# Cross-attention's DMA queue: a context chunk's transposing load directly behind its low part, ahead of the next context rows

## The chip, the cores and the metric

One core of a Trainium2 chip runs the kernel. The metric is the time of one execution in device microseconds (us); three executions of the kernel before took 1845.61 to 1848.7, with a median of 1846.81. Engines: TensorE (PE; its weight loads are PEld), VectorE (DVE), ScalarE (ACT), GpSimd (POOL) and SyncE (SP), which here issues nearly all DMAs. SPq in a row is SyncE's sequencer issuing one.

## What is computed

One decoder layer with the normalisation behind each part, on x (16 batches, 112 rows, 1024 columns) and a context (16 batches, 375 rows, 1024 columns), all in float32:

```
x = layernorm(x + attn(x))                    # q, k, v of width 256
x = layernorm(x + xattn(x, ctx))              # the part around the change
x = layernorm(x + ffn(x))                     # 1024 -> 2752 -> 1024, 4-bit weights, silu(gate) * up

xattn(text, features):
    Q = text @ Wq.T + bq;  K = features @ Wk.T + bk
    return softmax(Q @ K.T / sqrt(1024)) @ features
```

## The kernel before

The kernel writes each engine's instruction stream by hand; engines meet through semaphores, and within an engine order is the order written. To keep float32 accuracy with float16 matmuls it splits an operand into a high part (float16 of the scaled value) and a low part (what is left), and multiplies in three passes (high high, high low, low high).

Cross-attention is done one batch n at a time, 16 batches in all. Wq and Wk are multiplied together once into M, so that a batch's logits are (M x1) times the context. G = M x1 is made for pairs of batches in groups called g_chunk, four of them per batch, two batches ahead of use. The context of a batch has 375 rows, taken as three chunks of 128, 128 and 119 rows. For each chunk of each batch:

- SyncE loads the rows from DRAM (load_ctx, L2152; the third chunk as two DMAs, L2155 and L2156) into cx. There is one cx buffer per chunk, so the load of batch n+2 waits until the low part of the same chunk of batch n+1 has been made (semaphore s_cl).
- VectorE takes the largest absolute value of each row (context_max, L779); when all three chunks are there, TensorE and VectorE make a scale out of it (context_largest, context_factor).
- ScalarE writes the high part (context_hi, L1433), VectorE the low part (context_lo, L810), into cxp, which has two slots by the batch's parity.
- SyncE issues a transposing load from cxp to cxt, also two slots (load_cxt, L2178, a DMA_TRANSPOSE of 128 rows by 2048 float16, 512 KB). TensorE's logits (L1784; its matmuls show under the helper's line L1647) wait for all three of a batch (s_ct). The untransposed cxp is what the attended rows are made from.

VectorE's order while batch n is attended: normalise batch n-1, with the low part of chunk 0 of batch n+1 set in while a reciprocal root is fetched from GpSimd; low part of chunk 1 of n+1; softmax input of n (L771), which waits for the logits of n; low part of chunk 2 of n+1; largest of chunk 0 of batch n+2 (waits for its load); row_term of n+1; low part of the probabilities (L816), on which TensorE's attended rows wait; largest of chunks 1 and 2 of n+2; residual sum of batch n (add_attended, L901), which waits for the attended rows; scale of n+2. 

TensorE's order: logits of n, two g_chunks, transposed probabilities, a g_chunk, attended rows, the largest of the context of n+2 (L1744), a g_chunk.

SyncE's order for batch n is the function cross_attention that the diff touches (L2220). Before: for each chunk wait for its low part of n+1 and load the rows of batch n+2 into its place (after chunk 0 also store x2 of batch n-1, L2197); then wait for the logits of batch n-1, and issue the three transposing loads of batch n+1; then the transposing load of x2 of batch n-1 (L2202), the residual rows of batch n+2 (L2144), which wait for the residual sum of batch n, and in batches 0 to 2 two transposing loads of x1 (L2085). Batches 0 to 3 and 12 to 15 are written out, 4 to 11 are a loop of two turns of four. Batches 14 and 15 have no batch n+2 and load no context.

Of the kernel before, what the change touches and what calls it, by code (L numbers as in the profile page):

```python
# [40 lines left out]
def decoder_layer(nc, t_in, out):  # L41
# [19 lines left out]
    CC = len(CP)  # L61
# [28 lines left out]
    with ExitStack() as ctx:  # L90
# [289 lines left out]
        def rows(ap, n):  # L380

            return ap[bass.ds(n * S, S), :]
# [21 lines left out]
        def known(n, limit):  # L404

            return isinstance(n, int) and n < limit


        def batches(g, has):

            for b in range(GB):
                n = g * GB + b
                yield b, n, (lambda k, b=b: has or b + k < GB)
# [1630 lines left out]
        def _(sp):  # L2044
# [37 lines left out]
            def load_x1t(q):  # L2082

                for m in range(2 * q, 2 * q + 2):
                    sp.dma_start_transpose(x1t.rearrange("p l k t -> p (l k) t")[:, :, m * S:(m + 1) * S],  # L2085
                                           x1p_d[m * S:(m + 1) * S, :]).then_inc(s_x1t[q], 16)
# [56 lines left out]
            def load_residual(n, b):  # L2143
                sp.dma_start(xr3[0:S, b % 2, :], rows(x1_d, n)).then_inc(s_xr3[b % 2], 16)  # L2144
# [3 lines left out]
            def load_ctx(n, c):  # L2148

                base = n * CTX + c * P  # L2150
                if c < CC - 1:
                    sp.dma_start(cx[:, c, :], ctx_rows[bass.ds(base, P), :]).then_inc(s_cx[c], 16)  # L2152
                    return
                even = CP[c] // 16 * 16
                sp.dma_start(cx[0:even, c, :], ctx_rows[bass.ds(base, even), :]).then_inc(s_cx[c], 16)  # L2155
                sp.dma_start(cx[even:CP[c], c, :], ctx_rows[bass.ds(base + even, CP[c] - even), :]).then_inc(s_cx[c], 16)  # L2156
# [19 lines left out]
            def load_cxt(c, s):  # L2176

                sp.dma_start_transpose(cxt[s].rearrange("p l k t -> p (l k) t")[:, :, c * P:(c + 1) * P],  # L2178
                                       cxp[s][:, c, :, :].rearrange("p l d -> p (l d)")).then_inc(s_ct[s], 16)
# [14 lines left out]
            def store_x2(n, s):  # L2194

                sp.wait_ge(s_n, NB + n + 1)
                sp.dma_start(rows(x2_d, n), yo[0:S, s, :]).then_inc(s_yout[s], 16)  # L2197

            def load_x2t(n):

                sp.wait_ge(s_lo, n + 1)
                sp.dma_start_transpose(x2t.rearrange("p l k t -> p (l k) t")[:, :, bass.ds(n * S, S)],  # L2202
                                       x2p[0:S, :, :].rearrange("p l d -> p (l d)")).then_inc(s_x2t, 16)

            def load_chunk(i, s, w):

                for m, name in enumerate(("gate", "up")):

                    to = qw[s][m][:, 0:w] if w == P else qw[s][0][:, m * w:(m + 1) * w]
                    if known(i, 1):  # L2210
                        to = qw_first[m]
                    sp.dma_start(to, t_in[f"L0_ffn_{name}_qweight"][:, bass.ds(i * P, w)].bitcast(
                        U32)).then_inc(s_qw[s], 16)
                for r in range(4):
                    for lo, hi in ((0, 3 * GU), (3 * GU, 4 * GU)):
                        at = 0 if lo == 0 else P
                        sp.dma_start(tabc[s][32 * r + lo:32 * r + hi, :, at:at + w],
                                     tabr_d[:, lo:hi, bass.ds(i * P, w)].rearrange("m g c -> g m c")).then_inc(s_tc[s], 16)

            def cross_attention(g, more):  # L2220
                for b, n, has in batches(g, more):
                    if known(n, NB) and n == NB - 2:
                        load_chunk(0, 0, P)
                    for c in range(CC):
                        if has(1):
                            sp.wait_ge(s_cl, CC * (n + 1) + c + 1)
                        if has(2):
                            load_ctx(n + 2, c)
                        if c == 0 and not known(n, 1):
                            store_x2(n - 1, (b + 1) % 2)  # L2230
                    if has(1):
                        if not known(n, 1):
                            sp.wait_ge(s_l, n)
                        else:
                            sp.wait_ge(s_v, 2 * NG)
                        sp.sem_inc(s_due, 1)
                        for c in range(CC):
                            load_cxt(c, (b + 1) % 2)
                    if not has(1):
                        sp.wait_ge(s_l, NB)  # L2240
                        load_chunk(1, 1, P)
                    if not known(n, 1):
                        load_x2t(n - 1)
                    if has(2):
                        sp.wait_ge(s_y3, 2 * (n + 1))
                        load_residual(n + 2, (b + 2) % GB)
                    if known(n, 3):
                        load_x1t(5 + n)

            cross_attention(0, True)  # L2250
            with sp.Fori(1, NG - 1) as g:
                cross_attention(g, True)
            cross_attention(NG - 1, False)


# [186 lines left out]
```

## Time and profile before

| | |
|---|---|
| Median of 3 executions | 1846.81 us |
| Profiled execution | 1848.76 us, span 1847.0 us |
| PE busy | 1737.1 us, 94% of the span |
| DVE busy | 1069.9 us, 58% |
| ACT, POOL busy | 494.4 and 502.6 us, 27% each |
| TensorE's granted clock | 0.99 of full speed |
| Chain that ended last | PE 45%, issue 28%, DVE 11%, SPq 6%, DMA 5% |
| SPq L2178 (the transposing loads of the context) in that chain | 4% |

The span is read as busy time by engine and as a chain. Busy time says how full an engine is on average over stages that are limited by different things; the chain follows back from the last instruction to what released each step. The cross-attention stage runs from about 350 to 700 us. A wait in a row names the producer whose signal came last. Times of rows are microseconds from the start of the span; a mean of one instruction is in ns where it says so.

### The profile page before, as it was taken

The numbers are of one execution on the slowest core, as the hardware profiler recorded it, in microseconds if no ns is written. First come the engines' busy times: TensorE is split into PE (matmuls) and PEld (weight loads), VectorE is DVE, ScalarE is ACT, GpSimd is POOL, SyncE is SP. The second block draws the span as 40 slices with busy tenths as digits, with TensorE's granted clock in tenths as the row PEclk, the third lists the DMA queues.
The fourth block names the chain that finished last, engine by engine and source line by source line (L and its number), as shares of the span: only waits on it lengthen the run. The fifth ranks groups of instructions, "written<-read, shape, count | busy, mean of one in ns | idle before, by whom it ended". The sixth has DMA issues, their size and how long they took to land.

```text
span 1847.0 us, 26676 instructions
## 1 busy us (share of the span) xinstructions
PE 1737.1 (94%) x9784; PEld 979.2 (53%) x9784; DVE 1069.9 (58%) x1656; ACT 494.4 (27%) x734; POOL 502.6 (27%) x326
## 2 busy tenths in 40 slices
PE   5898899897899988998999999999999899999998
PEld 3666644486777754444444444444445344444443
DVE  7788550656788875667777777787775211111111
ACT  3222210354555543233323323233232100000000
POOL 0221378223333425543323223223231000000000
PEclk9999999999999999999999999999999999999999
DMA  9342571599999977763231321322313822122120
GB/s 324 102 130 80 158 205 34 120 209 231 225 236 239 232 166 156 179 143 80 56 88 48 81 62 48 95 48 62 81 45 79 324 101 107 53 106 106 53 106 23
DMA packets 335590, 231.89 MB, mean 126 GB/s; under 512 B 288224, under 2 KB 302624, under 8 KB 333348
## 3 DMA queue, kind: packets, MB, share of 16 engines
q1 hardware_dynamic: 329284, 227.85, 47.8%
q10 hardware_dynamic: 6240, 3.15, 0.6%
q8 instruction: 43, 0.70, 0.2%
q14 instruction: 23, 0.19, 0.0%
HBM read 122.93 MB, written 60.83 MB: 99 GB/s over the span
## 4 chain that ended last, share of the span: by engine, by line
PE 45%; issue 28%; DVE 11%; SPq 6%; DMA 5%; POOL 3%; ACT 1%; DVEq 0%; POOLq 0%; ACTq 0%
PE psum L1647 44%; SPq L2178 4%; DMA arena<-arena 3%; DMA arena<-in_x 2%; DVE arena L810 1%; POOL small L1162 1%; POOL arena L1171 1%; PE psum L1899 1%; PE psum L1825 1%; DVE arena L1016 1%; DVE arena L1014 1%; DVE arena L1011 1%; DVE arena L875 1%; DMA x_parts_scratch<-arena 1%; SPq L2085 1%
## 5 line engine op out<-in xcount | busy, mean ns | idle before, releaser
L1647 PE MATMUL psum<-arena 128*128 128x448 f16 (+6 forms) x7176 | 1273.0, 338 | 50.7 <-DMA arena<-arena 24.6
L1647 PEld LDWEIGHTS psum<-arena 128*128 128x128 f16 (+3 forms) x7176 | 752.3, 109 | 552.8 <-issue 89.4
L2002 PE MATMUL psum<-arena 128*128 128x512 f16 x1820 | 393.5, 379 | 6.4 <-DMA arena<-down_weights_scratch 3.7
L2002 PEld LDWEIGHTS psum<-arena 128*128 128x128 f16 x1820 | 177.7, 98 | 222.2 <-DMA arena<-down_weights_scratch 5.4
L1245 POOL TENSOR_TENSOR arena<-arena 128x1024 f16<-128x1024 f32 (+1 forms) x60 | 149.8, 2509 | 417.0 <-ACT arena L1456 417.0
L1144 DVE SCALAR_TENSOR_TENSOR arena<-psum,small,arena 128x512 f32<-128x512 f32 x28 | 20.9, 751 | 331.9 <-PE psum L2002 331.9
L1162 POOL TENSOR_TENSOR small<-small 112x1 f32<-112x1 f32 (+1 forms) x46 | 50.9, 1107 | 510.7 <-DVE small L471 510.7
L1547 ACT ACTIVATE arena<-arena,small 128x448 f32<-128x448 f32 x68 | 45.5, 668 | 208.6 <-DVE arena L1076 145.2
L1456 ACT ACTIVATE arena<-arena 128x1024 f16<-128x1024 f32 (+1 forms) x60 | 68.8, 1173 | 120.2 <-DVE arena L852 91.9
L1236 POOL TENSOR_TENSOR arena<-arena 128x224 f16<-128x224 f32 x64 | 55.6, 869 | 124.9 <-ACT arena L1427 124.8
L850 DVE TENSOR_TENSOR arena<-arena,psum 128x1024 f32<-128x1024 uint32 x65 | 79.1, 1217 | 2.9 <-PE psum L1825 0.9
L852 DVE TENSOR_TENSOR arena<-arena,psum 128x1024 f32<-128x1024 f32 x65 | 79.3, 1221 | 2.2
L1475 ACT ACTIVATE arena<-arena 128x448 f16<-128x448 f32 (+1 forms) x88 | 50.7, 576 | 103.7 <-DVE arena L864 103.7
L875 DVE TENSOR_TENSOR arena<-arena 128x448 f16<-128x448 f32 (+1 forms) x88 | 56.8, 646 | 36.8 <-ACT arena L1475 36.8
L779 DVE TENSOR_REDUCE small<-arena 128x1 f32<-128x1024 f32 (+1 forms) x48 | 58.0, 1216 | 26.5 <-DMA arena<-in_ctx 26.1
L810 DVE SCALAR_TENSOR_TENSOR arena<-arena,small 128x1024 f16<-128x1024 f32 (+1 forms) x48 | 61.2, 1279 | 12.0 <-ACT arena L1433 12.0
L1433 ACT ACTIVATE arena<-arena,small 128x1024 f16<-128x1024 f32 (+1 forms) x48 | 51.8, 1138 | 46.3 <-DVE small L806 46.3
L466 DVE BATCH_NORM_STATS2 small<-arena 112x6 f32<-112x512 f32 (+1 forms) x92 | 58.8, 681 | 1.4 <-DVE small L806 1.1
L482 DVE TENSOR_SCALAR arena<-arena,small 112x1024 f32<-112x1024 f32 (+1 forms) x46 | 44.3, 964 | 25.1 <-POOL small L1162 25.1
L864 DVE SCALAR_TENSOR_TENSOR arena<-arena,small 128x448 f32<-128x448 f32 (+1 forms) x72 | 49.0, 680 | 13.4 <-ACT arena L1484 10.6
L830 DVE TENSOR_TENSOR arena<-arena,small 128x1024 uint32<-128x1024 uint32 x43 | 55.8, 1297 | 0.3
L1252 POOL TENSOR_TENSOR arena<-arena 128x1024 f16<-128x1024 f32 x21 | 44.8, 2132 | 40.0 <-ACT arena L1464 40.0
(213 smaller groups left out, 1207.3 us busy)
## 6 DMA issues: line engine op xcount, KB each, us to landing
h_scratch<-arena SPq DMA_DIRECT2D x84, 224.0 KB, 2.9
arena<-h_scratch SPq DMA_DIRECT2D x13, 1376.0 KB, 6.0
arena<-in_ctx SPq DMA_DIRECT2D x32, 512.0 KB, 5.2
arena<-in_x SPq DMA_DIRECT2D x32, 448.0 KB, 5.6
x_scratch<-arena SPq DMA_DIRECT2D x32, 448.0 KB, 3.6
arena<-x_scratch SPq DMA_DIRECT2D x32, 448.0 KB, 4.7
arena<-in_L_ffn_down_qweight SPq DMA_DIRECT2D x21, 512.0 KB
down_weights_scratch<-arena SPq DMA_DIRECT2D x20, 512.0 KB, 3.8
```

The source lines that it names most:

```text
L466: dve.bn_stats(st[0:n, 6 * h:6 * h + 6], y[:, h * HALF:(h + 1) * HALF]).then_inc(s_st, 1)
L779: ins = dve.tensor_reduce(cmx[0:CP[c], c:c + 1], cx[0:CP[c], c, :], AX.X, ALU.max, apply_absolute_value=True)
L810: dve.scalar_tensor_tensor(cxp[b % 2][0:CP[c], c, 1, :], cx[0:CP[c], c, :], fc[0:CP[c], b:b + 1], cxp[b % 2][0:CP[c], c, 0, :], ALU.mult, ...
L850: dve.tensor_tensor(w, w.bitcast(U32), zeros, ALU.subtract).then_inc(s_dq, 1)
L852: dve.tensor_tensor(w, w, scales, ALU.mult).then_inc(s_wf if done is None else done, 1)
L875: dve.tensor_tensor(h_st[0:n, 1, cols], h_f[0:n, :], h_st[0:n, 0, cols], ALU.subtract).then_inc(s_hl, 1)
L1162: pool.tensor_tensor(rstd[0:n, :], ve[0:n, :], mhalf[0:n, :], ALU.pow).then_inc(s_rstd, 1)
L1245: return pool.tensor_tensor(dst[:, :, 1, :], wf32[:, lo * HALF:hi * HALF].rearrange("p (c n) -> p c n", n=P), dst[:, :, 0, :], ALU.subtract)
L1456: return act.activation(wgu[s][:, lo * 4:hi * 4, 0, :], wf32[:, lo * HALF:hi * HALF].rearrange("p (c n) -> p c n", n=P), ACT.Identity)
L1647: mm = pe.matmul(out, a, r, start=(k == 0), stop=(k == len(pairs) - 1))
L2002: mm = pe.matmul(bk[2 * s + c], ht[s][:, i, a, :], weights_of(i, w, c), start=(i == 0 and (w, a) == PASSES[0]), stop=(i == NI - 1 and (w, ...
L2178: sp.dma_start_transpose(cxt[s].rearrange("p l k t -> p (l k) t")[:, :, c * P:(c + 1) * P], cxp[s][:, c, :, :].rearrange("p l d -> p (l d) ...
```

## The change

On SyncE's queue, in cross_attention, the three transposing loads of batch n+1 are no longer a group behind the context loads of batch n+2. The wait for the logits of batch n-1 moves to the front, and inside the loop over chunks each chunk's transposing load follows directly behind the wait for its low part and ahead of the load of the same chunk of batch n+2. The counter s_due, which nothing waits for, is stepped per chunk. No other engine's stream changes.

```
                         load_chunk(0, 0, P)
-                    for c in range(CC):
-                        if has(1):
-                            sp.wait_ge(s_cl, CC * (n + 1) + c + 1)
-                        if has(2):
-                            load_ctx(n + 2, c)
-                        if c == 0 and not known(n, 1):
-                            store_x2(n - 1, (b + 1) % 2)
                     if has(1):
                         if not known(n, 1):
                             sp.wait_ge(s_l, n)
                         else:
                             sp.wait_ge(s_v, 2 * NG)
-                        sp.sem_inc(s_due, 1)
-                        for c in range(CC):
+                    for c in range(CC):
+
+                        if has(1):
+                            sp.wait_ge(s_cl, CC * (n + 1) + c + 1)
+                            sp.sem_inc(s_due, 1)
                             load_cxt(c, (b + 1) % 2)
+                        if has(2):
+                            load_ctx(n + 2, c)
+                        if c == 0 and not known(n, 1):
+                            store_x2(n - 1, (b + 1) % 2)
                     if not has(1):
```

## Rows read from the trace of the kernel before

**Rows 1.** Engines' busy us (count) by window: PE, PEld, DVE, ACT, POOL, PEclk, DMA share, GB/s
```profile
550.00:570.00 20.00, 18.64 (x153) 15.99 (x152) 16.99 (x33) 10.93 (x18) 7.33 (x6) 1.00 1.03 249
```

**Rows 2.** Waits, 470 to 645 us: who waited for whom, us, times, longest
```profile
PE psum L1647 <- DMA arena<-arena: 13.2, 9, 1.8
DVE logits L771 <- PE psum L1647: 7.0, 6, 3.1
DVE small L779 <- DMA arena<-in_ctx: 6.6, 11, 1.2
```

**Rows 3.** Chain that ended last, 549 to 592 us: start us, us, what
```profile
554.01 0.33 SPq L2155
...
554.95 3.77 SPq L2178
...
560.88 4.82 DMA arena<-arena
565.74 4.04 PE psum L1647 x24
569.81 0.68 DVE logits L771
...
585.22 4.04 PE psum L1647 x24
```

**Rows 4.** VectorE's timeline in the middle batches: start us, us, instruction, [idle before]
```profile
489.40 1.28 DVE L810 SCALAR_TENSOR_TENSOR arena<-arena,small 128x1024 f16<-128x1024 f32 x1
...
565.43 1.28 DVE L810 SCALAR_TENSOR_TENSOR arena<-arena,small 128x1024 f16<-128x1024 f32 x1
...
572.64 1.22 DVE L779 TENSOR_REDUCE small<-arena 128x1 f32<-128x1024 f32 x1 [0.40 <-DMA arena<-in_ctx]
...
577.45 1.22 DVE L779 TENSOR_REDUCE small<-arena 119x1 f32<-119x1024 f32 x1 [0.37 <-DMA arena<-in_ctx]
...
580.90 0.75 DVE L901 SCALAR_TENSOR_TENSOR arena<-psum,small,arena 112x512 f32<-112x512 f32 x1 [0.91 <-PE psum L1647]
...
584.43 1.28 DVE L810 SCALAR_TENSOR_TENSOR arena<-arena,small 128x1024 f16<-128x1024 f32 x1
...
603.90 1.28 DVE L810 SCALAR_TENSOR_TENSOR arena<-arena,small 128x1024 f16<-128x1024 f32 x1
```

**Rows 5.** SyncE's queue in one of those batches, same columns
```profile
566.91 0.36 SPq L2152 DMA_DIRECT2D arena<-in_ctx  x1
...
572.42 0.33 SPq L2155 DMA_DIRECT2D arena<-in_ctx  x1
...
573.35 8.73 SPq L2178 DMA_TRANSPOSE arena<-arena  x3
```

**Rows 6.** Transposing loads, all, then two of one batch; context loads: ns, landing us
```profile
L2178 SPq DMA_TRANSPOSE arena<-arena x31: 1803/3099/5673, 455.5 to 650.0; - x31
...
L2178 SPq DMA_TRANSPOSE arena<-arena x2: 2069/2283/2497, 558.8 to 560.9; - x2
...
DMA to landing us min/median/max: 4.5/4.6/4.8
...
DMA to landing us min/median/max: 3.4/5.2/7.4
```

**Rows 7.** SyncE and VectorE in batches 0 to 3, timeline
```profile
382.95 11.78 SPq L2178 DMA_TRANSPOSE arena<-arena  x3
...
404.79 1.21 SPq L2152 DMA_DIRECT2D arena<-in_ctx  x1
...
451.84 0.58 SPq L2152 DMA_DIRECT2D arena<-in_ctx  x1
...
394.00 2.33 DVE L779 TENSOR_REDUCE small<-arena 128x1 f32<-128x1024 f32 x2
...
399.03 0.75 DVE L901 SCALAR_TENSOR_TENSOR arena<-psum,small,arena 112x512 f32<-112x512 f32 x1 [1.09 <-PE psum L1647]
...
467.80 1.28 DVE L810 SCALAR_TENSOR_TENSOR arena<-arena,small 128x1024 f16<-128x1024 f32 x1
```

## The prediction, made before the result was known

> **What bounds the kernel now.** The queues touched here run only while cross-attention runs, some 350 to 700 us into the span, so I read windows of that stretch. First, busy time by engine: in 20 us TensorE is busy 18.6, VectorE 17.0, and the DMA engines' share is 1.03 [rows 1]. No engine has much to spare. Second, the waits between 470 and 645 us, nine batches: TensorE waits 13.2 us for a transposing load (9 times, so 1.5 a batch), VectorE 7.0 for logits and 6.6 for context rows [rows 2]. Third, the chain, which is one loop repeated: the low part of chunk 2, its context load, three transposing loads one behind the other, the landing of the third, 24 matmuls of logits, the softmax input, and then the next low part of chunk 2 [rows 3, 4]. All three transposing loads stand in that loop though two of them could have gone earlier. Fourth, VectorE and SyncE inside one batch [rows 4, 5]. A batch takes (603.90 - 489.40) / 6 = 19.1 us [rows 4].
>
> **What the change does in that loop.** It adds and removes nothing: 48 transposing loads and 64 context loads remain. For chunks 0 and 1 it pulls the transposing load ahead; for chunks 0, 1 and 2 it pushes the context load behind one, two and three transposing loads. The wait for the logits of the batch before, which now comes first, has long been met, and in batch 0 the wait that stands there is for self-attention; both cost nothing. Behind each transposing load stand also the store of x2 (chunk 0) and, after chunk 2, the transposing load of x2 and the residual load. The bookkeeping increments are free: increments aren't busy work and I bound them between nothing and 0.1 us a batch.
>
> I count from the end of the low part of chunk 0 at 565.43 + 1.28 = 566.71 [rows 4].
>
> Gained: TensorE's wait. After the change the third transposing load is issued at about 7.4 (below) and lands by 12.5, while TensorE only reaches those logits at 585.22 - 566.71 = 18.5 [rows 3], or a wait earlier. So the 1.5 us a batch are gone, and with them VectorE's wait for logits. By this alone a batch would take 19.1 - 1.5 = 17.6 us, TensorE's own work.
>
> Paid: the context rows. VectorE takes the largest of chunks 0, 1 and 2 of the context two batches on in the same batch, and already now waits for them: chunk 0's load is issued 0.2 after the low part and its reduction starts at 572.64, 5.9 from zero, after a wait; chunk 2's at 577.45, 10.7 from zero, again after a wait; its load was issued at 572.4, so it lands in 5.0 [rows 4, 5]. These loads have no cover at all.
>
> How long does a transposing load hold the queue? SyncE spends 8.73 us on three of them [rows 5]; one takes 1.8 us at least, 3.1 in the median, 5.7 at most [rows 6], and the long ones are those with other transfers still in flight ahead: the first of a group, behind context rows, took 3.77 [rows 3]. The second and third of that group took 2.1 and 2.5 and landed 2.4 us apart (558.8 + 4.5 and 560.88 + 4.82) [rows 3, 6]. The new queue, from zero:
> - 0.2: transposing load 0, nothing in flight ahead, 2.2 us. 2.4: context 0, which lands 5.2 later [rows 6], at 7.6, against 5.9 now.
> - 2.8: store of x2. 3.2: transposing load 1, now itself behind context rows and a store, so 3.8 us. 7.0: context 1, landing at 12.2; its reduction starts at about 9 now.
> - 7.4: transposing load 2 (its low part was ready at 5.5 and costs nothing), 2.3 us. 9.7: context 2, landing 5.0 later at 14.7, against 10.7.
>
> The last is what counts. From the start of chunk 2's reduction to the end of the next low part of chunk 0 lie 585.71 - 577.45 = 8.3 us, of which VectorE waits 0.9 for TensorE [rows 4]; that wait goes, since TensorE is done first. So a batch takes 14.7 + 7.4 = 22.1 us, **3.0 more** than 19.1. TensorE is then no longer the bound: its attended rows start behind the probabilities, about 1.7 later than now, and it has 4 us to spare. The bounds of the one uncertain term, where context 2 lands: from below, three issues at the least 1.8 and the least landing 3.4 [rows 6] give 0.2 + 5.4 + 1.2 + 3.4 = 10.2, and then TensorE's 17.6 us bind; from above, all three issues at 3.8 and the median landing 5.2 give 18, cycle 25.4. I take 14.7, because it is put together from the same sequence of transfers that the trace shows, where SyncE needs 8.7 for three; the bytes agree: three transposes, three chunks and a store are 3.4 MB, and at the 249 GB/s of the window [rows 1] they take 13.8 us.
>
> The Trainium skill speaks against this sum: Advanced Engine Details and Errata, section X-Bar Transpose (TRN2), says that transposing DMAs on trn2 are as fast as regular ones, 350 to 400 GB/s. The 2.4 us between two landings for 512 KB, 218 GB/s, contradict that for this shape. By the page's rate, as an estimate, each takes 1.4 us and context 2 lands about 3 us earlier, which leads to the last rival below.
>
> **The sum.** Ten batches (4 to 13) of the full loop: 10 x 3.0 = +30 us. Batches 14 and 15 load no context and are led by VectorE; the wait for logits of batch 14, under 1 us, is gained: -1. The first four, from their own rows [rows 7]: in batch 0 three transposing loads hold SyncE 11.8 us from 382.95, right behind context 2's load; moved ahead of it they push it to 382.5 + 11.8 = 394.3, landing 399.3, where its reduction (the second of the two that start at 394.00) starts at 395.2 now: 4.1, less the 1.1 that VectorE waits for TensorE there now, +3.0. In batches 0 to 2 SyncE also issues x1's transposing loads at the end and is itself the bound: context 0 goes out at 404.79 and two rounds later at 451.84, 23.5 us each. After the change the first transposing load goes out at 407.8, and the next round starts after context 2 has landed (14.7), its reduction (1.2), the residual sum (581.65 - 578.67 less the wait of 0.9: 2.1 [rows 4]), and residual and x1 loads (404.79 - 399.78 = 5.0): 23.0 later, 430.8, then 453.8. From there 22.1 to the end of the next low part of chunk 0: 475.9, against 467.80 + 1.28 = 469.1, +6.8 for the first four together. Total 30 + 6.8 - 1 = **+35.8 us**. All of it reaches the end, since gate and up start when x2 is there, and they are TensorE's work without gaps. The profiled execution took 1848.8 us around its span of 1847.0, 2 us over the median 1846.8 of the runs; 1848.8 + 35.8 = 1884.6 for it, and 1846.8 + 35.8 = 1882.6 against the median; I say **1882 us**.
>
> **The rivals.**
> - *A smaller loss.* If transposes issue in 2.2 us each even behind loads, context 2 goes out at 8.1 and lands at 12.7; a batch takes 20.1, +1.0. Ten of them and 2 for the start: +12, 1859 us. For it: the second and third of a group took 2.1 and 2.5 [rows 6]. Against: those had no context load right ahead.
> - *No change.* The DMA engines are the bound on both sides, share 1.03 [rows 1], and order doesn't matter: 1847 us. Against: the share also counts packets that wait, and VectorE's waits name transfers, not a full loop of them.
> - *Faster.* This is the gain without the price: transposing loads hold the queue 1.8 us and context rows land 4.0 after their issue. Context 2 then lands at 10.8, as now, and TensorE or VectorE bind at about 18.3: -0.8 in ten batches, and in the first four SyncE's rounds shrink from 23 to 19: together about -14, 1833 us. It decides where context 2 lands before 11.7 (11.7 + 7.4 = 19.1). For it: the 1.8 and 3.4 have been seen [rows 6], and the chain names the transposing loads [rows 3]. Against: three landings 2.4 apart alone make 7.2 us. This is also the outcome by the page's rule named above.
> - The change can't fail to act: the two are plain instructions of one queue.
>
> **How the numbers follow.** Forecast (1868 to 1900, context 2 landing at 13.7 to 16.5) 0.62; smaller loss 0.17; no change 0.07; faster 0.14. A difference of 0.2%, 3.7 us, is about what a measurement of this kernel can tell from none. Faster 0.14, same 0.07, slower 0.79. The range runs from the no-change case to the far end of the forecast: 1846 to 1900, leaving 0.14 below and some 0.05 above.
>
> **What the profile after would show.** Right: SyncE's timeline alternates transposing and context loads; TensorE's wait for the transposing loads is near nothing; VectorE's wait for context rows grows from 0.7 us a batch to about 5, most of it ahead of chunks 0 and 2; low parts of chunk 0 stand 22 us apart in the middle; busy shares of all engines fall. Wrong: reductions of chunk 2 starting less than 11.7 us after the low part of chunk 0, or transposing loads whose issue takes 1.8 us wherever they stand.

## The result and the profile after

The changed kernel takes 1918.2 us (median, 1915.7 to 1923.4) against 1847.8 before, a ratio of 1.0388 with an interval of 1.0365 to 1.041. It is slower, as forecast, but by 70 us and not by 36, outside the stated range. The profiled execution has a span of 1914.2 us, 67.2 more than before. Where a kernel ran more than once, its time and ratio are of fast executions; only the last one below had slow ones, two of twelve.

The page of the changed kernel: span, busy time of each engine, and TensorE's granted clock in 40 slices, which dips in the slices of this stage (before, every slice had a 9).

```profile
span 1914.2 us, 26706 instructions
...
PE 1767.5 (92%) x9784; PEld 995.1 (52%) x9784; DVE 1062.0 (55%) x1656; ACT 493.7 (26%) x734; POOL 503.3 (26%) x326
...
PEclk9999999998988888999999999999999999999999
```

Busy time by engine from 500 to 600 us, in the middle of cross-attention, first of the kernel before, then of the changed one (columns as in rows 1; the two short stretches belong to one batch):

```profile
500.00:600.00 100.00, 92.80 (x744) 78.85 (x743) 82.38 (x157) 59.21 (x95) 37.27 (x32) 1.00 1.04 234
```

The changed kernel:

```profile
500.00:600.00 100.00, 77.79 (x572) 64.30 (x572) 61.17 (x119) 43.90 (x72) 28.45 (x24) 0.90 0.80 176
620.00:626.00 6.00, 2.62 (x13) 1.29 (x10) 2.04 (x2) 1.85 (x3) 2.69 (x2) 0.91 0.96 228
626.00:633.00 7.00, 6.36 (x34) 5.26 (x35) 6.09 (x18) 3.63 (x5) 1.57 (x1) 0.59 0.34 90
```

TensorE is busy 15 us less in these 100, VectorE 21, and the data moved falls from 234 to 176 GB/s. The matmuls fall from 744 to 572, as they must if a batch takes 25.0 us in place of 19.35. Nothing took the place of the lost work: everything waits. The waits between 470 and 645 us, the counterpart of [rows 2], say for what:

```profile
DVE small L779 <- DMA arena<-in_ctx: 53.9, 20, 3.9
...
PE psum L1744 <- DVE small L784: 29.4, 7, 6.3
...
PE psum L1647 <- DVE arena L816: 6.5, 4, 2.8
...
DVE logits L771 <- PE psum L1647: 2.5, 3, 0.9
```

The wait of TensorE for transposing loads, 13.2 us before, is gone. VectorE's wait for context rows has grown from 6.6 to 53.9 us, over seven batches in place of nine: 7.7 us a batch, where it was 0.7 and about 5 was forecast.

The chain of the changed kernel in one batch, the counterpart of [rows 3]:

```profile
606.85 1.30 DVE arena L810
608.23 1.69 SPq L2178
...
611.98 4.66 SPq L2178
...
617.46 3.19 SPq L2178
620.86 0.42 SPq L2155
621.47 3.68 DMA arena<-in_ctx
625.18 1.23 DVE small L779
...
631.16 1.30 DVE arena L810
```

And VectorE's reductions of chunks 0 and 1 in it, the counterpart of [rows 4]; that of chunk 2 is in the chain:

```profile
614.81 1.22 DVE L779 TENSOR_REDUCE small<-arena 128x1 f32<-128x1024 f32 x1 [0.80 <-DMA arena<-in_ctx]
...
620.85 1.22 DVE L779 TENSOR_REDUCE small<-arena 128x1 f32<-128x1024 f32 x1 [3.13 <-DMA arena<-in_ctx]
```

From one low part of chunk 0 (606.85) to the next (631.16) lie 24.3 us. The chain runs through SyncE: transposing load 0 (1.69), context 0, store, transposing load 1 (4.66), context 1, transposing load 2 (3.19), context 2, its landing, VectorE's reduction, the scale and the next low part. Before, transposing loads and logits stood in the loop; now it is transposing loads and context rows. Over the ten batches 4 to 13 a batch takes 25.0 us, against 19.35 in the same ten before.

### The profile page after: what moved, and what is told of

Same layout as the page of the kernel before. It is cut to its first block, busy times and chain, and to the rows that moved or that the text cites. A ratio compares the mean times of both kernels' runs of the same rounds, so it can differ in the third digit from the quotient of the medians.

```text
span 1914.2 us, 26706 instructions
## 1 busy us (share of the span) xinstructions
PE 1767.5 (92%) x9784; PEld 995.1 (52%) x9784; DVE 1062.0 (55%) x1656; ACT 493.7 (26%) x734; POOL 503.3 (26%) x326
## 4 chain that ended last, share of the span: by engine, by line
PE 40%; issue 27%; SPq 12%; DVE 11%; DMA 5%; POOL 3%; ACT 1%; DVEq 0%; POOLq 0%; ACTq 0%
PE psum L1647 38%; SPq L2178 8%; DMA arena<-in_ctx 3%; SPq L2085 2%; DMA arena<-in_x 2%; DVE arena L901 1%; SPq L2152 1%; DVE small L779 1%; DVE small L466 1%; POOL arena L1171 1%; DVE arena L810 1%; PE psum L1899 1%; PE psum L1825 1%; POOL small L1162 1%; DVE arena L1016 1%
## 5 line engine op out<-in xcount | busy, mean ns | idle before, releaser
L1647 PE MATMUL psum<-arena 128*128 128x448 f16 (+6 forms) x7176 | 1297.7, 343 | 34.2 <-DVE arena L816 17.9
L1647 PEld LDWEIGHTS psum<-arena 128*128 128x128 f16 (+3 forms) x7176 | 767.6, 111 | 546.7 <-issue 99.4
L1744 PE MATMUL psum<-ident,small 128*128 128x128 f32 x32 | 10.0, 405 | 50.7 <-DVE small L784 50.7
L482 DVE TENSOR_SCALAR arena<-arena,small 112x1024 f32<-112x1024 f32 (+1 forms) x46 | 40.2, 874 | 27.3 <-POOL small L1162 27.3
```

Of the source, the lines that this page charges most:

```text
L1647: mm = pe.matmul(out, a, r, start=(k == 0), stop=(k == len(pairs) - 1))
```

## The experiments

Times are medians; a ratio is against the kernel before on the same chip, with its interval. "A batch" is the mean over the same ten batches. T is a transposing load, C a context load, S the store of x2. Before, a batch's queue is C S C C T T T; after the change T C S T C T C. Edits are shown in excerpts: those of 1 to 4, 7, 9 and 10 as made to the changed kernel, those of 6 and 8 to the kernel before.

**1. Small context loads, in both orders.** Two theories stood at first: A, that the issue of a transposing load doesn't end before plain transfers ahead of it have landed, and B, that it is stretched by the bytes in flight.

```
+                if few:
+                    for at in range(0, 16 if c < CC - 1 else 32, 16):
+                        sp.dma_start(cx[at:at + 16, c, :], ctx_rows[bass.ds(base + at, 16), :]).then_inc(s_cx[c], 16)
+                    return
...
-                            load_ctx(n + 2, c)
+                            load_ctx(n + 2, c, True)
```

In the changed order:

> The changed kernel, but inside the batch loop every context load brings 16 rows (32 of the third chunk) in place of 128 or 119, so most of the context is stale and the output isn't the layer's. Theory A (hold): SyncE's issue of a transposing load doesn't end before plain transfers issued ahead of it have landed, however small; then the transposing load of chunk 1, 0.6 us behind the store of x2, still takes 3.5 us or more, and that of chunk 2, behind a small load, 2.5 to 3.3; the median over all stays above 2.6. Theory B (bytes): the issue is stretched by the bytes still in flight; then all but the one behind the store take 1.7 to 2.2 and the median is about 2.0. Both: VectorE's waits for context rows shrink from 117 us to under 40, and the time falls from 1918 to under 1870.

In the order before:

> The kernel before with the same small context loads in the loop (output not the layer's). It is the partner of the changed kernel with small loads. Theory A: the first transposing load of each group, behind a small load, falls from 3.8 to 2.5 to 3.0; theory B: to 2.0. With the price of context rows gone, the order of the change should be the better one: this one takes 1835 to 1845, the changed one with small loads 5 to 20 us less. If the changed order is still slower with small loads, the price is not that context rows land late.

Measured, one execution each: 1880.5 us in the changed order (a batch 21.7), 1830.3 in the order before (a batch 18.3); both expectations of a time were missed (under 1870, and 1835 to 1845). With small loads the changed order still costs 50 us, where a gain of 5 to 20 was expected: most of the price is not the bytes of the context rows. The expectation would go further, that the price is then not that context rows land late. That does not follow: between 470 and 645 us VectorE still waits 40.6 us for them, since they go out late. SyncE's queue in the changed order, with small loads:

```profile
610.30 0.35 SPq L2201 DMA_DIRECT2D x_scratch<-arena  x1
610.83 3.60 SPq L2182 DMA_TRANSPOSE arena<-arena  x1
...
615.25 1.83 SPq L2182 DMA_TRANSPOSE arena<-arena  x1
```

A transposing load behind the store of x2 takes 3.60 us (median 3.8), one behind 16 rows 1.83 (median 1.8). A fails on the second, having asked for 2.5 to 3.3 behind a small load; B had 1.7 to 2.2 for all but the one behind the store, which fits. In the order before, the first of a group takes 1.83 in the median, where A had 2.5 to 3.0 and B 2.0. So this experiment speaks for B; experiment 2, and 6 by the landings, speak against it.

**2. Context load first, then the transposing load, chunk by chunk** (C T S C T C T).

```
                         if has(1):
                             sp.wait_ge(s_cl, CC * (n + 1) + c + 1)
+                        if has(2):
+                            load_ctx(n + 2, c)
+                        if has(1):
                             sp.sem_inc(s_due, 1)
                             load_cxt(c, (b + 1) % 2)
-                        if has(2):
-                            load_ctx(n + 2, c)
```

> Per chunk the context load first and the transposing load directly behind it, all else as in the change. Theory A (a transposing load behind a plain load is held until that has landed, about 4 us each): context 1 goes out at about 5, context 2 at about 10 after the low part of chunk 0 and lands at 14.4; a turn takes 21.9 us against 25.0 after the change and 19.3 before, and the kernel about 1881. Theory B (it is only that context loads stand behind transposing loads, each 2.2 us): context 2 goes out at 6 and lands at 11; the kernel takes 1838 to 1850.

Measured 1888.9 us, ratio 1.0226 (1.0192 to 1.026), a batch 22.4. This is A's number (1881) within 8 us and far from B's (1838 to 1850). Context rows stand behind one transposing load less than after the change, and most of the loss remains.

**3. Only chunk 0's transposing load moved** (T C S C C T T).

```
                         if has(1):
                             sp.wait_ge(s_cl, CC * (n + 1) + c + 1)
-                            sp.sem_inc(s_due, 1)
-                            load_cxt(c, (b + 1) % 2)
+                            if c == 0:
+                                sp.sem_inc(s_due, 1)
+                                load_cxt(0, (b + 1) % 2)
...
+                    if has(1):
+                        for c in range(1, CC):
+                            load_cxt(c, (b + 1) % 2)
```

> Only chunk 0's transposing load goes ahead of its context load; those of chunks 1 and 2 stay behind the context loads. Theory A: with nothing in flight ahead it takes 1.7 us, context 0 lands at 6.3 after the low part (5.9 before), contexts 1 and 2 as before; of the two left, only the first is held. The third transposing load lands at 14.8, before TensorE asks: the wait of 1.5 us a turn goes, and the kernel takes 1832 to 1842. Rival (each transposing load moved ahead costs its share of the 70 us): about 1870.

Measured 1866.4 us, ratio 1.0088 (1.0066 to 1.0111), a batch 20.2: slower, where A's sum gave a gain. SyncE's queue and VectorE's reductions in one batch:

```profile
597.66 2.07 SPq L2178 DMA_TRANSPOSE arena<-arena  x1
599.94 0.67 SPq L2152 DMA_DIRECT2D arena<-in_ctx  x1
...
603.21 0.33 SPq L2155 DMA_DIRECT2D arena<-in_ctx  x1
...
604.68 1.22 DVE L779 TENSOR_REDUCE small<-arena 128x1 f32<-128x1024 f32 x1 [1.64 <-DMA arena<-in_ctx]
...
608.48 2.36 DVE L779 TENSOR_REDUCE small<-arena 128x1 f32<-128x1024 f32 x2 [0.89 <-DMA arena<-in_ctx]
```

The transposing load is cheap here, 2.07 us, as A says. But context 0 goes out 2.4 us behind the low part's end at 597.56 and lands at 604.68, 7.1 from it (5.9 before), and the three context loads and the store now go out within 4 us and arrive bunched. Context 1, out at 601.47, lands 7.0 later at 608.45, 10.9 from the low part's end where it was 8.3 before, and VectorE waits 0.89 for it; context 2 is reduced behind it, from about 609.6. The sum had kept both landings as they were. This is also only half of the loss: of the 19.6 us by which the profiled span grew, 8 lie in the ten batches and 9.1 in the four before them, which were not looked into.

**4. One transposing load ahead of context 2 only** (C S C T C T T).

```
+                        if has(1) and c == 1:
+                            sp.sem_inc(s_due, 1)
+                            load_cxt(0, (b + 1) % 2)
```

> One transposing load (chunk 0) is issued behind context loads 0 and 1 and ahead of context 2; the other two stay behind context 2. Theory A: it is held until context 1 has landed, some 4 us; context 2 goes out at 7.3 after the low part of chunk 0 and lands at 11.8 against 10.7, the two left take 3.8 and 2.1, and TensorE's wait goes: a batch takes 19.3 us, the kernel 1842 to 1858. If the price is per transposing load moved ahead (a third of 70 us), about 1870.

Measured 1861.3 us, ratio 1.009 (1.0062 to 1.0118), a batch 20.6; the transposing load in the middle takes 4.8 us (median of ten; 4 expected). The forecast was 3 us too low at its upper end, and the batch 1.3 us too short (19.3). Moving one load costs 15 to 18 us in either place.

**5. Context loads on ScalarE's queue**, with the transposing loads as after the change and as before it.

```
+                    if has(2):
+                        load_ctx(n + 2, 1)
                     act.wait_ge(s_lm, n + 1)
...
                         g_out(KC + 4 * n + 1, 4 * (b % 2) + 1, 1 - b // 2)
+                        load_ctx(n + 2, 2)
                     probs_hi(n)
...
                     if has(3):
+                        load_ctx(n + 3, 0)
```

(here load_ctx waits for its s_cl and issues with act.dma_start; on SyncE the calls are taken out)

> The change, but the context loads of the batch loop are issued from ScalarE's queue (chunk 1 ahead of the exponential, chunk 2 behind the next copy of G, chunk 0 of the next batch at the end of a batch), each behind the same wait for its low part. SyncE keeps the transposing loads per chunk, the stores and the residual. Theory A1 (a transposing load is held by plain transfers ahead of it on its own queue): transposing loads of chunk 2 fall from 3.5 to 1.8 us, that of chunk 1, behind the store of x2, stays at about 3.7; context rows no longer stand behind them and VectorE waits for them as before the change (0.7 us a batch) or less; TensorE's wait is gone, a batch takes 17.8 to 18.5 us and the kernel 1830 to 1840. Theory A2 (it is held by whatever the DMA engines have in flight, on any queue): they stay at 3.5 and more, context rows still no longer stand behind them, so 1838 to 1855. If context rows land late because of bytes and not because of the queue, the time stays above 1880.

> The kernel before, with the context loads of the batch loop on ScalarE's queue as in the run beside it; the three transposing loads stay one group behind the last low part. Theory A1: the group no longer stands behind context 2 and takes 1.8 + 2.1 + 2.3 instead of 8.7 us, so the third lands 2 us earlier and TensorE's wait of 1.5 a batch nearly goes: 1832 to 1845. Theory A2: the group still takes 8 to 9 us: 1845 to 1855. If the run beside it isn't faster than this one, moving transposing loads ahead gains nothing even where context loads are out of the way.

Measured 1920.4 us, ratio 1.0396 (1.0359 to 1.0432), with the transposing loads moved, and 1859.6, ratio 1.0087 (1.006 to 1.0115), with them grouped. The second is 5 us above A2's range; its group of three takes 10.1 us in the median of batches 4 to 13 (8.9 in the kernel before), far from A1's 6.2. The first is far from A1's and A2's numbers; it falls to the third case, above 1880, which was to mean bytes. SyncE's queue, ScalarE's queue and VectorE's third reduction in one batch of it:

```profile
618.66 4.34 SPq L2196 DMA_TRANSPOSE arena<-arena  x1
623.26 0.36 SPq L2215 DMA_DIRECT2D x_scratch<-arena  x1
623.81 11.97 SPq L2196 DMA_TRANSPOSE arena<-arena  x2
...
618.75 0.38 ACTq L1493 DMA_DIRECT2D arena<-in_ctx  x1
...
624.33 0.38 ACTq L1496 DMA_DIRECT2D arena<-in_ctx  x1
...
624.88 0.86 ACTq L1497 DMA_DIRECT2D arena<-in_ctx  x1
...
636.44 1.22 DVE L779 TENSOR_REDUCE small<-arena 119x1 f32<-119x1024 f32 x1 [7.45 <-DMA arena<-in_ctx]
```

Transposing load 0 takes 4.34 us, with a context load issued 0.1 us later on the other queue, where it took 1.8 in the median in experiment 3; its issue ends at 623.00 and that context load lands at 623.20. Then two transposing loads take 11.97 us, and context 2, issued at 624.33 and 624.88 behind nothing on its own queue but context 1 (down at 626.3), is not used before 636.44, when they are through; VectorE waits 7.45 for it. The bytes don't explain this: from 624 to 636 the DMA engines move 185 GB/s, where the kernel before moved 234 in the stage. So A1 falls: a transposing load isn't held by its own queue's plain transfers alone, and plain loads on another queue don't get past it.

**6. The two kinds by themselves**, in short sequences behind the kernel's end.

```
+                rows_in(0)
+                turned(0)
+                all_landed()
...
+                for c in range(2):
+                    rows_in(c)
+                    turned(c)
+                all_landed()
```

(rows_in loads 128 context rows, turned is the transposing load, all_landed waits for both)

> The kernel before, and behind its last store, with everything else idle, short sequences on SyncE's queue, each awaited before the next, three times over: a transposing load (T, 128 x 2048 float16, as for a context chunk) alone; a load of 128 context rows (C) alone; T T T; C T; T C; a load of 16 rows and T; C C T; C C T T; C T C T. Theory A (T is held until the plain transfers ahead of it have landed): T alone issues in 1.7 to 1.9 us; behind C in 3.4 to 4.2, which is C's landing less its issue; behind 16 rows in 1.8 to 2.2; behind C C in 4.5 to 5.5; C T C T takes 3 us longer to its last landing than C C T T. Theory B (only bytes in flight count, each kind at its rate): T behind C 2.2 to 3.0, behind C C 3.5 to 4.5, and C T C T takes as long as C C T T within 0.7 us. Both: T T T issues at 2.0 to 2.4 each.

SyncE's timeline: T alone (1846.73), T T T (1854.52), C T (C at 1863.76), C C T T (1887.72), C T C T (1897.71; the C at 1911.79 comes behind one more T, awaited).

```profile
1846.73 2.15 SPq L2426 DMA_TRANSPOSE arena<-arena  x1
...
1854.52 6.76 SPq L2426 DMA_TRANSPOSE arena<-arena  x3
1863.76 0.34 SPq L2422 DMA_DIRECT2D arena<-in_ctx  x1
...
1887.72 0.82 SPq L2422 DMA_DIRECT2D arena<-in_ctx  x2
...
1897.71 0.34 SPq L2422 DMA_DIRECT2D arena<-in_ctx  x1
...
1911.79 0.34 SPq L2422 DMA_DIRECT2D arena<-in_ctx  x1
```

Single DMAs, their issue in ns (min/median/max), start and landing: T of C T, the landing of its C, T of C C T, the landing of its second C.

```profile
L2426 SPq DMA_TRANSPOSE arena<-arena x1: 3430/3430/3430, 1864.1 to 1864.1; - x1
...
DMA to landing us min/median/max: 5.4/5.4/5.4
...
DMA to landing us min/median/max: 3.9/3.9/3.9
...
L2426 SPq DMA_TRANSPOSE arena<-arena x1: 4522/4522/4522, 1881.1 to 1881.1; - x1
...
DMA to landing us min/median/max: 6.6/6.6/6.6
...
DMA to landing us min/median/max: 5.1/5.1/5.1
```

In C T, C is issued at 1863.76 and lands after 3.9, at 1867.7; T's issue starts at 1864.14 and ends after 3.43, at 1867.6. In C C T the second C is issued at 1880.7 and lands at 1885.8; T's issue ends at 1881.14 + 4.52 = 1885.7. In C T C T both T end about 0.1 us before their C's landing too (1898.10 + 3.40 against 1897.71 + 3.9; 1902.16 + 3.35 against 1901.54 + 4.1). In all 15 cases of the three rounds, the issue of a transposing load directly behind 128 rows ends within 0.2 us of their landing. **The issue of a transposing load ends when the plain load ahead of it has landed**, and it lands itself 2.0 us later. Behind 16 rows, which land in 2.2, the load takes 1.7 to 1.9, as alone: this is why experiment 1 saw nothing there. The store of x2 is nearly as large as a context chunk (448 against 512 KB), and in the changed kernel held the next one as a chunk does: 611.98 + 4.66 = 616.64, and the store landed at 616.55.

The trace shows that the same holds behind another transposing load. In T T T the second issue ends at 1858.92 and the first load lands at 1858.93; the third ends at 1861.28 and the second lands at 1861.35. All nine such issues of the probe end within 0.3 us of the landing ahead, and so do, within 0.6 us, all twenty that stand second or third in the groups of batches 4 to 13 of the kernel before. In the order before with small loads one second issue took 3.61 us, ending at 601.93, though only loads of 16 rows stood ahead of the group; the first load landed at 602.11. So a transposing load behind another costs 2.3 us or so because the one ahead lands that much later, and behind a plain load 3.4 because that takes longer to land.

A's last point fails: C T C T is no longer than C C T T (1907.5 against 1897.7 - 1887.7 = 10.0; 1907.5 - 1897.7 = 9.8). Alternating costs no throughput, as B had it. What it moves is when C lands: C C T T has its second C down after 5.7 us, C T C T after 7.9.

**7. Two transposing loads as a pair ahead of all context loads** (T T C S C C T).

```
+                        for c in range(2):
+                            sp.wait_ge(s_cl, CC * (n + 1) + c + 1)
+                            sp.sem_inc(s_due, 1)
+                            load_cxt(c, (b + 1) % 2)
...
+                        load_ctx(n + 2, 0)
...
+                        load_ctx(n + 2, 1)
...
+                        load_ctx(n + 2, 2)
...
+                        load_cxt(2, (b + 1) % 2)
```

> The transposing loads of chunks 0 and 1 go as a pair behind the low part of chunk 1, ahead of context loads 0, 1 and 2; that of chunk 2 stays behind context 2. Nearly as many transposing loads stand ahead of the context loads as in the change (2, 2, 2 against 1, 2, 3), but the queue alternates between the two kinds twice a batch and not three times. If the price is the alternation: the pair takes 2.0 each with nothing in flight, contexts go out at 6.7 and behind, context 2 lands at about 13, a batch takes 20.5 us and the kernel 1853 to 1870. If it is the place behind transposing loads as such, context 0 lands at 11.5 against 8 after the change and the time stays at 1895 or above.

Measured 1918.8 us, ratio 1.0371 (1.0352 to 1.039), a batch 24.8: as slow as the change, with fewer alternations and one load less moved. SyncE's queue and VectorE's first reduction in one batch:

```profile
611.34 4.56 SPq L2178 DMA_TRANSPOSE arena<-arena  x2
616.12 0.69 SPq L2152 DMA_DIRECT2D arena<-in_ctx  x1
...
618.23 1.15 SPq L2155 DMA_DIRECT2D arena<-in_ctx  x1
...
621.05 1.22 DVE L779 TENSOR_REDUCE small<-arena 128x1 f32<-128x1024 f32 x1 [4.68 <-DMA arena<-in_ctx]
```

TensorE's wait for the low part of the probabilities (L816) from 470 to 645 us:

```profile
PE psum L1647 <- DVE arena L816: 36.5, 7, 6.1
```

Here the late one is context 0: out at 616.12, it is used at 621.05, 9.8 after the low part's end at 611.25, and VectorE waits 4.68 for it. Row term and probabilities stand behind that reduction, TensorE waits 36.5 us for them, and the attended rows come late. So place decides, not the number of alternations: any context load that comes late stops VectorE. (The forecast had context 0 at 11.5.)

**8. The store of x2 behind the transposing loads**, in the kernel before (C C C T T T S).

```
-                        if c == 0 and not known(n, 1):
-                            store_x2(n - 1, (b + 1) % 2)
...
                             load_cxt(c, (b + 1) % 2)
+                    if not known(n, 1):
+                        store_x2(n - 1, (b + 1) % 2)
```

> The kernel before with the store of x2 moved from between context loads 0 and 1 to behind the three transposing loads. 448 KB fewer are in flight when the transposing loads come. If these bytes hold the first of them, the group falls from 8.7 to about 8 us and the kernel takes 1838 to 1845; if only the context load right ahead does, it takes 1844 to 1851 as before, and with the store now behind transposing loads and ahead of that of x2 it may lose 5.

Measured 1845.9 us, ratio 0.9994 (0.9979 to 1.0008): no change. In the batch of [rows 5] the store goes out at 568.15 and lands at 573.72, while the group's first issue runs from 573.35 to 577.17: the store is down 3.4 us before that issue ends, and context 1, behind it in the queue, lands later still (575.05). So the store was not what the group waited for.

**9. The change with chunk 2's transposing load put back** (T C S T C C T).

```
                         if has(1):
                             sp.wait_ge(s_cl, CC * (n + 1) + c + 1)
-                            sp.sem_inc(s_due, 1)
-                            load_cxt(c, (b + 1) % 2)
+                            if c < CC - 1:
+                                sp.sem_inc(s_due, 1)
+                                load_cxt(c, (b + 1) % 2)
...
+                    if has(1):
+                        load_cxt(CC - 1, (b + 1) % 2)
```

> The change with one transposing load put back: that of chunk 2 stays behind context 2, those of chunks 0 and 1 stay ahead. Theory A (a transposing load is held until the plain load right ahead of it has landed, and what stands behind it waits that long): context 2 goes out 3.5 to 4 us earlier and lands 1.4 behind context 1 and not 4.3; a batch takes 22.0 to 22.5 us against 25.0, the kernel 1885 to 1895. Rival (bytes moved past, 2.3 us for one transposing load): a batch takes 23 or more, the kernel 1898 to 1905. If the price is the alternation from plain to transposing, 3 times a batch in both, the kernel stays at 1910 or above.

Measured 1888.5 us, ratio 1.0225 (1.0202 to 1.0248), a batch 22.3: A's number on all three counts. In one batch:

```profile
612.58 4.39 SPq L2178 DMA_TRANSPOSE arena<-arena  x1
617.17 0.42 SPq L2152 DMA_DIRECT2D arena<-in_ctx  x1
617.85 0.33 SPq L2155 DMA_DIRECT2D arena<-in_ctx  x1
...
618.72 4.17 SPq L2178 DMA_TRANSPOSE arena<-arena  x1
...
623.25 1.22 DVE L779 TENSOR_REDUCE small<-arena 119x1 f32<-119x1024 f32 x1 [0.32 <-DMA arena<-in_ctx]
```

Context 2 goes out 0.7 us after context 1, not 4.0, and its reduction follows the one before with a wait of 0.32. The transposing load left behind it is held for 4.17 us, and nobody waits for that.

**10. VectorE's row term ahead of the largest of chunk 0**, in experiment 3's order and in the order before.

```
+                    if has(1):
+                        row_term(n + 1, (b + 1) % GB)
                     if has(2):
                         context_max(n + 2, 0)
-                    if has(1):
-                        row_term(n + 1, (b + 1) % GB)
```

> Only chunk 0's transposing load ahead of its context load, as in the run chunk0_only, and on VectorE the row term of the next batch now comes ahead of the largest of chunk 0 and not behind it. If the loss of chunk0_only runs through VectorE's wait for context 0 and, behind it, the low part of the probabilities, the 1.2 us of the row term fill that wait: 1848 to 1858 against 1866. If it runs through context 2 alone, the time stays at 1860 or above.

> The kernel before with the same exchange on VectorE, row term ahead of the largest of chunk 0. VectorE waits 0.4 us there in some batches, so at most 0.4 a batch is to be had: 1841 to 1847. It is what the exchange does by itself.

Measured 1859.0 us, ratio 1.0061 (1.0042 to 1.0081), and 1847.3, ratio 0.9999 (0.998 to 1.0018). The first lies between the two expectations, and its interval overlaps that of experiment 3 (1.0066 to 1.0111), so whether the wait for context 0 carries part of that loss stays open; a batch is as long as there, 20.05 against 20.16, and in the two profiled executions most of the difference lies ahead of batch 4, whose first low part starts at 470.5 in place of 476.9. No version that computes the layer beat the kernel before.

## Why the prediction was half right

**What held.** The loop was read right: TensorE's wait for transposing loads goes (13.2 us to none), VectorE waits for context rows in its place, and the end of the loop from chunk 2's reduction to the next low part of chunk 0 is 7.3 us (625.18 to 631.16 + 1.28) where 7.4 was put. The last batches gave back 0.8 where 1 was put. The whole delay reached the end: 68.0 us at batch 14's first low part (661.3 to 729.3), 67.2 in the span. One sign was misplaced: VectorE waits for chunks 1 and 2 (3.1 us each), not for chunks 0 and 2.

**What failed is the term "context 2 lands at 14.7".** In the batch shown it is used at 625.18 - 608.13 = 17.0, and in one that takes 25.7 at 18.3. Step by step in that batch: transposing load 0 had 2.2 and took 1.69; transposing load 1 had 3.8 and took 4.66 (median 4.5), since the store ahead of it lands later than context 0; transposing load 2 had **2.3 and took 3.19** (median 3.5), and each context load itself held SyncE for 0.4 to 1.1, where the sum had 0.4. Context 2 so went out at 12.7 and not at 9.7, and landed in 4.3 and not 5.0. Of the 3.0 us by which it went out late, 0.9 came from each of transposing loads 1 and 2, 1.9 from the plain issues and the gaps of 0.2 us or so between issues, and transposing load 0 gave back 0.6. Context 0's issue alone took 1.06, directly behind a transposing load, where it took 0.36 before; in the probe a plain load in that place took 0.58 to 1.14 against 0.34. The sum had no term for this. The 2.3 was the mistake in reasoning: the prediction gave 3.8 to a transposing load behind a plain one and then took the third for one behind another transposing load, although context 1 stood right ahead of it. Experiment 9 takes just that load back and gains 30 us (1918.2 to 1888.5), 2.7 a batch, which is what the load costs in that place as a whole and not only what was missing from the 2.3; experiment 6 gives the rule behind it.

Two checks had seemed to carry the 14.7. The bytes by the rate of the window before, 13.8 us, assumed that the order doesn't change the rate; it fell from 234 to 176 GB/s. (They are 3.4 MB only if a MB is 1024 x 1024 bytes; in the unit of the 249 GB/s they are 3.6, and take 14.3 us.) The 8.7 us for a group of three was carried over as a sum, though two of its three loads had another transposing load right ahead, and after the change none has.

**The sum.** Ten batches: 3.0 each were put and 5.7 came (25.0 against 19.35; the forecast had 19.1 from six of these batches), +56.6 us in place of +30. First four: the end of batch 4's first low part moved from 469.1 to 480.4, +11.4 in place of +6.8. That this came near is in part luck: the first transposing load of the second round went out at 403.5 and not at 407.8, and the three rounds from there took 26.8, 25.0 and 25.6 us where 23.0, 23.0 and 22.1 were put. 56.6 + 11.4 - 0.8 = 67.2. The upper bound given for a batch, 25.4 us, was close to the truth for the middle batches (25.0 in the mean, 26.0 at most), but the range took only 16.5 of its 18.

**The rivals.** Smaller loss, no change and faster all took a transposing load for as cheap behind a context load as behind another or by itself, or left the order out; experiment 6 has 3.4 against 2.3 and 1.8. The smaller loss was also summed wrongly: context 2 out at 8.1 and landing 5.0 later is 13.1, a batch of 20.5 and not 20.1, which would make it 1863 us. The faster rival was also what the Trainium skill's Advanced Engine Details and Errata, section X-Bar Transpose (TRN2), would give. That transposing is as fast as regular DMAs isn't what the probe shows: in T T T landings are 2.4 us apart for 512 KB each, 218 GB/s, and in C C T the two plain loads land 1.7 us apart. The larger price here is the hold, which no rate contains.

**Left open.** Why the issue is held, and by what, was not found; experiment 5 shows that another queue doesn't avoid it. Why two transposing loads take 12 us there wasn't settled either: the first of them lands only 12.8 us after its issue, at 636.6, about when context 2 is down, and the second's issue ends at 635.78, 0.8 before it. Nor was it found why a plain load's issue is longer behind a transposing load, or what moving loads costs in the first four batches.

## What to carry to other kernels

Look at what stands right ahead of a transposing load on the chip, not at the queue's sum: it holds its queue until the transfer ahead has landed, and all that is queued behind it waits as long. Put plain loads that someone will wait for ahead of a group of transposing loads, and keep the group together, even if the wait for the last of them is the one that the chain names: no order tried here that splits the group was faster. A chain names the wait that ends last now; before moving work past other transfers, check whether their consumer already waits for them: here VectorE did, for 0.7 us a batch, and that was the warning.

## What the runs showed of the hardware

- A transposing load of 512 KB directly behind a plain load of 512 KB: issue 3.3 to 3.6 us, ending within 0.2 us of the plain load's landing; alone 1.5 to 2.2; behind two plain loads 4.5 to 4.8, ending with the second's landing; behind another transposing load 1.9 to 2.7, ending within 0.3 us of its landing (all in the probe).
- A plain load of 512 KB directly behind a transposing load: issue 0.58 to 1.14 us in the probe, against 0.34 by itself.
- Plain loads on ScalarE's queue beside transposing loads on SyncE's (experiment 5): two transposing loads took 11.97 us of issue, one context load 12 us from issue to use.
- TensorE's clock: in the changed kernel it idled for 4 us before each L1744, and in the stretch from 626 to 633, behind one of these, the granted clock was 0.59 of full speed, where it was 1.00 in the middle of the stage before. VectorE waited only 2.5 us for logits in 175, and the chain from 600 to 640 us has no piece of TensorE's, so the loss isn't the clock's.
